# Out-projection of a fused attention and feed-forward kernel: from one exact fp32 product to three fp32r products, with the low parts of the feed-forward sums moved between engines

## The reference

```python
att = softmax(einsum('blhd,bmhd->blmh', q, k) * scale, axis=2)
opt = einsum('blmh,blhd->blhd', att, v).reshape(b, l, d)   # v of the row's own token
return opt @ w_out.T + b_out                               # the out-projection
...
inter = relu(x @ wi.T + wi_b + lora); expert_out = inter @ wo.T + wo_b
x = x + layernorm(attention(layernorm(x)))
x = x + layernorm(ffn(layernorm(x)))
```

## Time and profile before

| What | us |
|---|---|
| median of 3 runs (516.14 to 516.30) | 516.17 |
| the profiled execution, time | 516.16 |
| the profiled execution, span of its instructions | 514.1 |
| TensorE busy | 500.0 |
| VectorE busy | 460.3 |
| ScalarE busy | 446.8 |
| GpSimd busy | 344.0 |

### The profile page before, as it was taken

One profiled execution on the slowest core, in us unless ns is written; L12 is line 12 of the kernel. 1 busy time (PEld: TensorE's weight loads), 2 busy tenths in 40 slices (PEclk: granted clock), 3 DMA queues, 4 the chain that ended last, 5 costly groups with the idle time before them and its releaser, 6 DMA issues.

```text
span 514.1 us, 8917 instructions
## 1 busy us (share of the span) xinstructions
PE 500.0 (97%) x2752; PEld 412.4 (80%) x2752; DVE 460.3 (90%) x1013; ACT 446.8 (87%) x1222; POOL 344.0 (67%) x514
## 2 busy tenths in 40 slices
PE   9999999999999999999999999999999999998995
PEld 6757555788898879888898879887888888777995
DVE  4799999997999899999999899999999799985555
ACT  3499999999999999999999999999999989993320
POOL 5698048317892898569883989478883966796171
PEclk9999999999999999999999999999999999999998
DMA  7783264017210635026320635035400760310002
GB/s 233 223 214 98 73 173 124 1 47 200 67 57 2 155 92 164 1 70 177 96 70 1 165 94 153 1 99 147 124 1 14 190 168 0 84 41 1 1 0 83
DMA packets 22690, 47.62 MB, mean 93 GB/s; under 512 B 5266, under 2 KB 13586, under 8 KB 22004
## 3 DMA queue, kind: packets, MB, share of 16 engines
q1 hardware_dynamic: 21956, 45.95, 33.6%
q0 software_dynamic: 256, 0.52, 0.4%
q10 hardware_dynamic: 432, 0.59, 0.4%
HBM read 8.24 MB, written 4.19 MB: 24 GB/s over the span
## 4 chain that ended last, share of the span: by engine, by line
PE 71%; ACT 13%; DVE 8%; POOL 4%; issue 1%; POOLq 0%; ACTq 0%
PE pu L201 38%; PE ps L229 16%; ACT ps L520 11%; DVE nmax L699 5%; PE pu L300 4%; PE ps L208 2%; PE ps L201 2%; PE pu L241 2%; PE pu L345 2%; POOL inter L1095 1%; DVE st L751 1%; PE pu L324 1%; ACT oT L545 1%; POOL xb L1022 1%; POOL y L1016 1%
## 5 line engine op out<-in xcount | busy, mean ns | idle before, releaser
L520 ACT ACTIVATE ps<-ps,nmax 128x512 f32<-128x512 f32 x512 | 345.7, 712 | 15.0 <-DVE nmax L699 14.4
L699 DVE TENSOR_REDUCE nmax<-ps 128x1 f32<-128x512 f32 x512 | 323.0, 679 | 18.8 <-PE ps L229 17.7
L229 PE MATMUL ps<-stack 128*128 128x512 f32 x512 | 178.4, 411 | 0.2
L520 ACT ACTIVATION_READ_ACCUMULATOR ps<-ps,nmax 128x1 f32 x512 | 132.3, 258 | 0.0
L229 PEld LDWEIGHTS ps<-stack 128*128 128x128 f32 x512 | 91.9, 189 | 16.8 <-ACT ps L520 4.2
L201 PEld LDWEIGHTS pu<-wo_r,inter 128*128 128x128 f32 x744 | 95.2, 188 | 4.9 <-POOL inter L1095 1.1
L201 PE MATMUL pu<-wo_r,inter 128*128 128x256 f32 x744 | 97.3, 282 | 0.9 <-POOL inter L1095 0.9
L201 PE MATMUL pu<-yT,wi_r 128*128 128x512 f32 x336 | 87.4, 395 | 0.0
L201 PEld LDWEIGHTS pu<-yT,wi_r 128*128 128x128 f32 x336 | 63.2, 188 | 14.6
L208 PE MATMUL ps<-ones_r 128*128 128x512 f32 x132 | 55.3, 458 | 3.3 <-ACT ps L520 2.2
L201 PE MATMUL pu<-xnT,wqk_r 128*128 128x512 f32 x186 | 47.5, 393 | 0.0
(11 more groups left out here) (167 smaller groups left out, 661.3 us busy)
## 6 DMA issues: line engine op xcount, KB each, us to landing
stack<-qk SPq DMA_DIRECT2D x256, 128.0 KB, 2.5
xb<-in_x SPq DMA_DIRECT2D x7, 512.0 KB, 3.7
out_y<-xb SPq DMA_DIRECT2D x7, 512.0 KB, 3.5
xb<-in_wo SPq DMA_DIRECT2D x1, 1024.0 KB, 7.0
vo<-in_wi SPq DMA_DIRECT2D x2, 512.0 KB, 6.2
oT<-in_wqk ACTq DMA_DIRECT2D x1, 512.0 KB, 4.1
xb<-in_x SPq DMA_DIRECT2D x4, 128.0 KB, 4.1
stack<-qk SPq DMA_DIRECT2D x8, 64.0 KB, 2.4
```

The lines of the kernel that those rows point to most:

```text
L229: e.matmul(ps[i % NS][:], st[:, 1 - p, c, t * 128:(t + 1) * 128], st[:, 2, c, :], start=True, stop=True).then_inc(scored, 1)
L520: e.activation(ps[i % NS][:], ps[i % NS][:], ACT.Exp, bias=nmax[:, i % 8:i % 8 + 1], accum_out=ssum[:, b % 2, t, h:h + 1]).then_inc(exped, 1)
L699: e.tensor_reduce(nmax[:, i % 8:i % 8 + 1], ps[i % NS][:], AX_X, ALU.max, negate=True).then_inc(maxed, 1)
```

## The change

Five edits go together.

1. `oT` and `wout_s` are gone. `wout_r` holds the high and low parts of the out-projection's weights, which GpSimd makes once, in batch 0, from a stage in `y[:, 2:4]`. `project` calls `three`.
2. The turned sums need parts too: ScalarE's `o_t` writes the high part, and a new `o_t` on VectorE the low part. Both lie in the buffer of the turned norm, `yT` (in `xnT` for batch 7). ScalarE's copy now also waits until TensorE has finished the last `f1` of the batch before, which reads that buffer.
3. `f1_last` is gone. Results 6 and 7 are staged like the others (in `y2`), and GpSimd makes the parts of all four pairs. `f2`'s second half waits for the fourth pair.
4. `gT`, which lay in `oT`, gets a tensor of its own; the stage of `wqk` moves to `vo`.
5. The lists of all engines and `FULL` are written anew.

```diff
-IDLE, FULL = (25, 3, 4), (4, 6, 15, 21, 26, ..., 118, 121, 126)      # 28 numbers, 18 of them from 64 up
+IDLE, FULL = (25, 3, 4), (9, 12, 21, 26, 33, ..., 116, 120, 124)     # 31 numbers, 21 of them from 64 up
...
-        oT = sb("oT", [128, 2, L])
-        wout_s = sb("wout_s", [128, 2, D])
+        wout_r = sb("wout_r", [128, 2, 2, D], F32R)
+        gT = sb("gT", [80, L])[:]
...
 tensor:
-                          e.wait_ge(oT_here, 2 * b + (u + 1 if b == B - 1 else 2))
+                          e.wait_ge(oT_low, 2 * b + (u + 1 if b == B - 1 else 2))
                     o = bank_of["y", b, u][:, k * 256:(k + 1) * 256]
-                    for c in range(2):
-                        p = e.matmul(o, oT[:, c, t * 128:(t + 1) * 128], wout_s[:, c, :], start=c == 0, stop=c == 1)
+                    oT = xnT if b == B - 1 else yT
+                    p = three(o, lambda a, c: oT[:, a, c, t * 128:(t + 1) * 128], lambda a, c: wout_r[:, a, c, :], (0, 1),
+                              True, True)
 scalar:
             def o_t(b, c):
                     e.wait_ge(oT_ps, 2 * b + c + 1)
-                    e.activation(oT[:, c, :], bank_of["oT", b, c][:], ACT.Copy).then_inc(oT_here, 1)
+                    if b:
+                        e.wait_ge(f1_ps, 8 * b)
+                    e.activation(yT[:, 0, c, :], bank_of["oT", b, c][:], ACT.Copy).then_inc(oT_high, 1)
             def f1(b, f):
-                    if f >= 6:
-                        e.activation(inter[:, 0, f, :], bank_of["f1", b, f][:], ACT.Relu).then_inc(f1_last_high, 1)
-                        return
-                    if f == 4:
-                        e.wait_ge(f1_pool_low, 3 * b + 1)
+                    if f in (4, 6):
+                        e.wait_ge(f1_pool_low, 4 * b + f // 2 - 1)
 vector:
+            def o_t(b, c):
+                    e.wait_ge(oT_high, 2 * b + c + 1)
+                    low(yT[:, 1, c], bank_of["oT", b, c], yT[:, 0, c], oT_low)
-            def f1_last(b, f):
-                    e.wait_ge(f1_last_high, 2 * b + f - 5)
-                    e.scalar_tensor_tensor(inter[:, 1, f, :], bank_of["f1", b, f][:], 0.0,
-                                           inter[:, 0, f, :].bitcast(F32), ALU.max, ALU.subtract).then_inc(f1_last_low, 1)
 pool:
+            e.tensor_copy(wout_r[:, 0], wout_st).then_inc(wout_split, 1)
+            e.tensor_tensor(wout_r[:, 1], wout_st, wout_r[:, 0].bitcast(F32), ALU.subtract).then_inc(wout_split, 1)
             for b in range(2, B - 1):
-                scale(b - 1), f1_lows(b - 2, 1, 0), x_norm(b + 1), y_norm(b - 1, HALVES[0])
+                scale(b - 1), f1_lows(b - 2, 1, 0), x_norm(b + 1), f1_lows(b - 2, 1, 1), y_norm(b - 1, HALVES[0])
```

More of the change, by code:

```diff
@@ L284, in o_t @@
                 if here(b):
-                    bank = banks[take(("oT", b, c), oT_here, 2 * b + c + 1)]
+                    bank = banks[take(("oT", b, c), oT_low, 2 * b + c + 1)]
                     e.wait_ge(scaled, 4 * b + 4)
@@ L725, in value, with o_half @@
                                     bf[:, 0, :].unsqueeze(1).to_broadcast([128, 2, D]), ALU.add).then_inc(v_here, 1)
+            def o_t(b, c):
+                if here(b):
+                    e.wait_ge(oT_high, 2 * b + c + 1)
+                    low(yT[:, 1, c], bank_of["oT", b, c], yT[:, 0, c], oT_low)
+            def o_half(h):
+                b = B - 1
+                e.wait_ge(oT_high, 2 * b + h + 1)
+                e.tensor_tensor(xnT[:, 1, :, cols(h)], parts(bank_of["oT", b, h]), xnT[:, 0, :, cols(h)].bitcast(F32),
+                                ALU.subtract).then_inc(oT_low, 1)
             def y_t(b, c):
@@ L968, in vector @@
-            b = B - 1
-            slot(0), ratio(b - 1), ratio_whole(b - 1), slot(1), slot(2), f1_last(b - 2, 6), slot(3), slot(4)
-            slot(5), slot(6), slot(7), slot(8), f1_last(b - 2, 7), project(b - 1, 0), slot(9)
-            y_stats(b - 1, HALVES[0]), y_aggr(b - 1, HALVES[0]), slot(10), project(b - 1, 1), slot(11)
-            y_stats(b - 1, HALVES[1]), slot(12), slot(13), y_aggr(b - 1, HALVES[1]), slot(14), slot(15), slot(16)
-            slot(17), sum_stats(b - 1, HALVES[0]), slot(18), sum_aggr(b - 1, HALVES[0]), slot(19), slot(20)
@@ new lines, in vector @@
+            slot(39), q_k(b + 1, 2), slot(40), value(b + 1, 0), slot(41), slot(42), slot(43), slot(44)
+            q_k(b + 1, 1), slot(45), slot(46), slot(47), slot(48), q_k(b + 1, 3), slot(49), slot(50), slot(51)
+            slot(52), slot(53), slot(54), slot(55), slot(56), slot(57), slot(58), slot(59), slot(60)
+            value(b + 1, 1), slot(61), slot(62), slot(63)
+            b = 1
+            ratio(b - 1), ratio_whole(b - 1), slot(0), slot(1), slot(2), x_stats(b + 1), slot(3), x_aggr(b + 1)
@@ new lines, in vector @@
+            b = B - 1
+            slot(0), ratio(b - 1), slot(1), ratio_whole(b - 1), slot(2), slot(3), slot(4), slot(5), o_t(b - 1, 0)
+            o_t(b - 1, 1), slot(6), slot(7), slot(8), slot(9), project(b - 1, 0), y_stats(b - 1, HALVES[0])
+            slot(10), y_aggr(b - 1, HALVES[0]), slot(11), slot(12), project(b - 1, 1), slot(13), slot(14)
+            y_stats(b - 1, HALVES[1]), y_aggr(b - 1, HALVES[1]), sum_stats(b - 1, HALVES[0]), slot(15), slot(16)
+            sum_aggr(b - 1, HALVES[0]), slot(17), slot(18), slot(19), slot(20), slot(21)
@@ new lines, in vector @@
+            y_aggr(b, HALVES[1]), norm(1, 1, y, y, b, HALVES[1]), y_half(0), add(1, y, b, HALVES[1])
+            sum_stats(b, HALVES[1]), sum_aggr(b, HALVES[1]), norm(2, 1, y, xb[:, b % XB], b, HALVES[1])
+            gate_half(1, 0), gate_half(2, 0), y_half(1), gate_half(3, 0), gate_half(1, 1), gate_half(2, 1)
+            gate_half(3, 1), f1_half(0, 0), y2_stats(b - 1, HALVES[0]), f1_half(0, 1), f1_half(0, 2), f1_half(0, 3)
+            f1_half(1, 0), y2_aggr(b - 1, HALVES[0]), y2_stats(b - 1, HALVES[1]), y2_aggr(b - 1, HALVES[1])
@@ L995, in pool @@
+            f1_half(1, 1), f1_half(1, 2), f1_half(1, 3), last_stats(0), last_stats(1), norm(3, 2, y2, y2, b, (0,))
+            add(3, y2, b, (0,)), norm(3, 2, y2, y2, b, (1,)), last_stats(2), norm(3, 2, y2, y2, b, (2,))
+            add(3, y2, b, (1,)), last_stats(3), add(3, y2, b, (2,)), norm(3, 2, y2, y2, b, (3,))
+            add(3, y2, b, (3,))
         def pool(e):
```

318 lines of the change are left out of this document (151 added, 167 removed).

## The result

The changed kernel takes 530.2 us (median of 4 runs, 529.9 to 531.5); the kernel before takes 516.15 us (4 runs on the same chip, 515.99 to 516.3). The ratio is 1.0279, 95% interval 1.0267 to 1.0291. The prediction had 513.4 with 510.3 to 517.0. The profiled run of after has a span of 528.3 us, 14.2 more than before.

The account below looks back on a forecast made before the run. TensorE was taken as the bound, with ScalarE and VectorE 1.3 and 1.9 us behind in a middle batch. The sum was 516.16 - 3.0 - 0.8 + 0.5 - 0.4 + 0.9 = 513.4 us, range 510.3 to 517.0.

Parts of the forecast that it names:

- Batch 0 "unchanged": First batch, led by the exponentials and without out-projection: taken as unchanged.
- The products, -3.0: Projection in five middle batches: 0.60 us less TensorE work each, -3.0 us; bounds 0 and -3.0.
- The start of a batch, -0.8: Middle batches up to the projection: half of a score's 0.33 us wait goes, -0.8 us; projection effectively 0.06 late.
- GpSimd's pair at nothing: Fourth pair of low parts on GpSimd, 3.5 us ahead of y_norm: idle time and slack absorb it, no cost.
- GpSimd takes the gain: Rival, chance 0.16: 0.66 us of the fourth pair appear at y_t, middle batches give back 0.60; 516.6 us.
- the projection waits for the low parts: Rival, chance 0.15: TensorE idles 1.2 us more per middle batch for VectorE, against 0.60 saved; 520.2 us.
- Cheaper products: Rival, chance 0.05: projection's six records take 0.65 us a tile, not 0.71; 1.3 us more gain, 512.1 us.
- Batch 1, +0.5: Batch 1: two added VectorE low parts +1.2, three fewer idle matmuls -0.7; +0.5 us.
- Batch 7, -0.4: Batch 7 before the scores end: TensorE saves 0.60 and 0.30, others are nearly full; -0.4 us, bounds 0 and -0.9.
- The end, +0.9: Behind the last exponential: projection 0.2 earlier, its tiles 0.3 less, uncovered f2 unit 1.42; +0.9 us, bounds 0 and +3.5.
- The fall of the clock: Sign of a wrong forecast: granted clock below 1.00 after the end's two waits before the projection, about 1.8 us each.

Follow-up runs that it names:

- both experiments: ScalarE's q_k(1, 0) put back behind slot 30 in the changed kernel: 526.4 us; the same step moved to behind slot 24 in the kernel before: 521.9 us.
- after_no_fourth: Changed kernel with ScalarE's q_k(1, 0) back behind slot 30 and GpSimd's fourth-pair subtraction over one column in batches 3 to 6: 525.8 us.
- after_dose: Changed kernel with one extra GpSimd copy ahead of the fourth pair's subtraction in the middle loop's batches: 536.7 us.
- products_only: Kernel before with only the projection as three fp32r products, with VectorE's low parts; GpSimd still makes three pairs: 527.9 us.
- before_no_last: Kernel before with VectorE's f1_last over one column in batches 3 to 6: 515.75 us.
- products_own6: products_only with the parts of batch 6's turned values in xnT instead of yT: 527.2 us.

## Why the prediction was wrong, step by step

- **Batch 0 "unchanged"** is the step that failed most: +5.8 of 14.2. The list of ScalarE moves a step that waits for transfers ahead of six slots, and I had followed queue by queue only the batches with a projection. The wait of 5.09 and both experiments show it.
- **The products, -3.0,** are the term of the sum that failed. The size of a tile was right: in batch 4 of after the three tiles in a row, 18 products, start at 253.83 (row below), and the next score at 255.98, 2.15 us for three, 0.72 each. The value was wrong: the saving doesn't reach the end of a batch, because behind the projection VectorE is as full as TensorE, 15.98 of 16 us. The bound "0, if another engine takes the place at once" was the truth. I had read the 1.9 us between the engines' sums over 56.8 us as room, and there was none in the 16 us that mattered.
- **The start of a batch, -0.8.** The sign was wrong. From `slot(0)` to the projection TensorE takes 5.52 us in after and took 4.88 before; less the 0.23 of the one more score that is 0.4 late, not 0.06. It doesn't wait at the projection, but at slot 8's score ahead of it, longer than the 0.36 before:

```profile
253.49 0.50 PE L229 MATMUL ps<-stack 128*128 128x512 f32 x1 [0.65 <-ACT ps L519]
253.83 2.32 PE L201 MATMUL pu<-wout_r,yT 128*128 128x256 f32 x18
```

- **GpSimd's pair at nothing.** The gap of 1.41 went as forecast, and from `scale` to the end of `sum_norm` GpSimd takes 26.90 us instead of 26.16, close to the 0.66 of the prediction. But `scale` starts only 0.28 us earlier against TensorE's `slot(0)`, and the step was then the first bound of the batch: 0.20 us of the 0.50 (after_no_fourth), and one to one for more in batches 4 and 5 (after_dose). The rival *GpSimd takes the gain* had the right mechanism and place: after's turn waits 0.28 us for it. The rival *the projection waits for the low parts* is what the change does without its new lists: 1.52 us of wait in products_only, well over its 0.6, and +1.19 a batch where it said +0.6, since the 0.60 of the products did not come off. So both rivals priced their loss against a gain that was not there.
- **Cheaper products**, six records in 0.65 us, is ruled out: 0.71. The count of the Trainium skill (FP8 and Floating Point Precision, TensorE Precision Notes), four passes for true fp32, does not give the saving of three products here; the trace's 0.86 and 0.71 do.
- **Batch 1, +0.5**: measured +0.56. products_only has +1.22 there, the two low parts in full, with the idle matmuls of the kernel before. The three fewer idle matmuls and the new lists bring it back to +0.56; they were not tried apart, so that the sum came out is not proof of its terms.
- **Batch 7, -0.4**: measured +2.55. The term took TensorE's saving of 0.9 and looked at how full the others are, not at what TensorE would wait for: 5.0 us of named waits where there were 0.3. In products_only VectorE's low parts make 1.1 us and the shared buffer up to 1.7; in after no run tells the waits' shares apart.
- **The end, +0.9**: measured +2.07. The mis-sized term is the 0.96 us of ScalarE's copies, which I took off behind the last exponential though they lay ahead of it. The projection starts 4.20 us behind it (478.50 to 482.70), not 3.48: the low part's 0.7. With 1.42 for the uncovered unit and -0.3 for the products that makes +1.8; 0.2 are left over. The fall of the clock that the prediction's last paragraph named as a sign came in some executions only, as the last section tells.

What runs have shown of after's 14.2 us: 4.5 are ScalarE's step in batch 0, 0.2 in each of batches 3 to 5 GpSimd's pair, and 1.8 of the 2.1 of the end can be read off its chain. Not settled: 1.2 us of batch 0, the 0.84 of batch 2, the other 0.3 of each middle batch, all of which lies behind `y_t` (31.12 against 30.82 in the table above), and how batch 7's loss divides. No version that does all the work beat the kernel before.

## What to carry to other kernels

Where three engines are each over 95% busy, an engine's share of a batch doesn't tell what its work is worth: look at windows of ten or so microseconds around the edit, and if a second engine is full just behind it, cost the saving at zero. The Trainium skill (Perfetto Trace Analysis, Identifying the Most-Contended Engine) says to optimize the engine with the highest occupancy first, but to judge TensorE by its arithmetic rate and the share of its weight loads, not by its matmul share. I had gone by the matmul share, 97%; by the weight loads TensorE has 80%, and VectorE, with 90%, is first. The runs bear out a part of that: 0.6 us less for TensorE left the batch 0.2 us longer until VectorE had room. But 1.2 us less for VectorE alone brought 0.07 (before_no_last), so the highest share didn't name what to shorten either. When two executions are compared, look at their granted clocks first: the 1.7 us that products_own6 had won were hidden by a fall of the clock. When an edit comes with new lists, go through every step that waits for a transfer, in every batch, the untouched ones first: one such step, moved six slots ahead, cost more than all the arithmetic was meant to bring.
